# A value scale found ahead of V Wo', keys split in another way, and four idle matmuls, in a fused attention and feed-forward kernel

## The reference, cut to what matters

```python
q = hidden @ Wq.T + bq
scores = einsum('bshd,hmd->bshm', q, memory_keys) / sqrt(128)
probs = softmax(scores)
mem_out = einsum('bshm,hmd->bshd', probs, memory_values)
x = layernorm(x + mem_out @ Wo.T + bo)
...
h = silu(tlin(x, w1)) * tlin(x, w2); h = gelu(tlin(h, h1)); h = gelu(tlin(h, h2))
x = layernorm(x + tlin(h, w3))
```

## Time and the profile before

| | |
|---|---|
| median of 3 runs | 1182.92 us (1181.91 to 1184.15) |
| profiled execution, its own time | 1182.86 us |
| its span in the trace | 1180.9 us |
| mean granted clock of PE | 0.971 |
| busy: PE, DVE, ACT, POOL | 1096.5, 971.5, 901.0, 664.0 us |

### The profile page before, as it was taken

How to read it: one execution, slowest core, us unless ns; L and a number is a source line. 1 busy time by engine, 2 the same in 40 slices (tenths; PEclk the granted TensorE clock), 3 DMA queues, 4 the chain that set the end, 5 groups by cost and what they waited for, 6 DMA issues and landing times. The chain is left out here.

```text
span 1180.9 us, 20085 instructions
## 1 busy us (share of the span) xinstructions
PE 1096.5 (93%) x5312; PEld 758.9 (64%) x5312; DVE 971.5 (82%) x1766; ACT 901.0 (76%) x1582; POOL 664.0 (56%) x614
## 2 busy tenths in 40 slices
PE   7589999999999999999999999643999999999996
PEld 5356666666666666666666666212788888888885
DVE  5868889998999998999899998465678878888875
ACT  5668778887887887887888888613788888888883
POOL 1278787887887887887888787772012112112110
PEclk9889999999999999999999999975999999999998
DMA  5578888888888888888888888812000100101000
GB/s 174 129 167 199 197 190 196 201 196 197 202 196 196 201 197 196 202 196 196 202 196 202 197 198 190 208 65 75 19 28 28 53 27 27 53 27 38 25 10 27
DMA packets 81922, 162.96 MB, mean 138 GB/s; under 512 B 19296, under 2 KB 44768, under 8 KB 81888
## 3 DMA queue, kind: packets, MB, share of 16 engines
q1 hardware_dynamic: 81888, 162.55, 57.9%
HBM read 19.87 MB, written 8.39 MB: 24 GB/s over the span
## 5 line engine op out<-in xcount | busy, mean ns | idle before, releaser
L271 POOL TENSOR_TENSOR pT<-slot_p,pT 128x512 f16<-128x512 f32 x512 | 587.6, 1182 | 139.9 <-ACT pT L310 139.9
L399 DVE TENSOR_SCALAR_CACHE_REDUCE rows<-s_ps 128x1024 f32<-128x1024 f32 x256 | 313.3, 1224 | 76.7 <-PE s_ps L464 62.0
L310 ACT ACTIVATE pT<-slot_p 128x512 f16<-128x512 f32 x512 | 296.9, 616 | 93.4 <-DMA slot_p<-rows 57.3
L363 DVE STREAM_TRANSPOSE rows<-rows 128x1024 f32<-128x1024 f32 x256 | 317.3, 1240 | 2.9 <-ACT rows L301 2.8
L462 PE MATMUL s_ps<-keys,q_buf 128*128 128x512 f32 x512 | 295.6, 577 | 11.6 <-DVE rows L399 6.6
L301 ACT ACTIVATE rows<-rows,bias 128x1024 f32<-128x1024 f32 x256 | 291.6, 1139 | 7.8 <-DVE bias L405 5.6
L489 PE MATMUL o_ps<-pT,v_hi 128*128 128x512 f16 x512 | 201.5, 393 | 34.8 <-POOL pT L271 32.1
L840 PE MATMUL ring<-h_hi,keys 128*128 128x512 f32 x512 | 203.7, 398 | 2.0 <-DVE h_lo L747 1.7
L464 PE MATMUL s_ps<-keys,q_buf 128*128 128x512 f32 x512 | 204.3, 399 | 0.0
L463 PE MATMUL s_ps<-keys,q_buf 128*128 128x512 f32 x512 | 202.8, 396 | 0.0
L841 PE MATMUL ring<-h_lo,keys 128*128 128x512 f32 x512 | 200.5, 392 | 0.0
(11 more groups left out here) (82 smaller groups left out, 1179.7 us busy)
## 6 DMA issues: line engine op xcount, KB each, us to landing
slot_p<-rows SPq DMA_DIRECT2D x1024, 128.0 KB, 2.3
x_in<-in_xT SPq DMA_DIRECT2D x32, 128.0 KB, 2.1
o_scratch<-o_sum SPq DMA_DIRECT2D x32, 128.0 KB, 1.9
o_in<-o_scratch SPq DMA_DIRECT2D x16, 256.0 KB, 2.8
x_in<-in_x SPq DMA_DIRECT2D x16, 256.0 KB, 3.1
out<-y_out SPq DMA_DIRECT2D x16, 256.0 KB, 2.4
slot_p<-in_kT SPq DMA_DIRECT2D x4, 512.0 KB, 6.0
slot_p<-in_vT SPq DMA_DIRECT2D x4, 512.0 KB, 8.4
```

Source lines behind the costliest of these rows:

```text
L271: nc.gpsimd.tensor_tensor(halves(s % RING, 1), slots_first(pp, s), halves(s % RING, 0), ALU.subtract).then_inc(split, 1)
L310: nc.scalar.activation(halves(s % RING, 0), slots_first(pp, s), ACT.Copy).then_inc(highed, 1)
L363: nc.vector.transpose(row_piece(tile, k), row_piece(tile, k)).then_inc(turned, 1)
L399: nc.vector.tensor_scalar(row_piece(tile, k), s_ps[:, j % 2, :], 1.0, None, ALU.mult, ALU.max, accum_out=part_max[:, tile, k:k + 1]).then_ ...
```

## The change

1. **Scale.** The scale is no longer found from v. ACT sums |V| over all slots for each of the 128 input channels while V is loaded (four passes, Abs with an accumulator; what they write goes to pT and isn't read). DVE adds the four. ACT multiplies |Wo'| by these sums per partition, PE multiplies by ones and so adds over the channels, and every partition has for each output column a bound on |V Wo'|. DVE clamps it, keeps the exponent, takes the reciprocal and scales Wo' by it: one power of two for each column instead of one for all. PE transposes the powers, so that column 0 of it is v_unscale per partition.
2. **V.** v comes out of PE scaled. Its eight halves move from steps 8 to 15 of frame 0 to steps 11 to 15 of frame 0 and 0 to 2 of frame 1. ACT copies each twice from PSUM, as 16-bit v_hi and as v_raw; POOL subtracts at once. L334, L337, L386, L417, L258 and L420 to L426 are gone.
3. **Keys.** The first piece is loaded and split in two halves; all low parts are made by DVE: three ahead of its first move, one behind each of the first two. One counting semaphore k_split stands for the four.
4. **PE** does four idle products of wq and x_in into o_ps behind the first query product. The x of pair 1 is loaded after them and behind V in SP's queue.

```diff
+        def value_halves(f, t):
+            step = t - V_STEP + STEPS * f if isinstance(f, int) else -1
+            return (step,) if 0 <= step < HALVES else ()
+        def k_part(t, n):
+            return half_piece(t, n) if n < 2 else piece(t, n - 1)
...
 # SP
+                if is_step(pair, 1):
+                    sp.wait_ge(warmed, 1)
-            for n in range(PIECES):
-                sp.dma_start(piece(k_raw, n), piece(kT, n)).then_inc(k_loaded[n], 16)
+            for n in range(K_PARTS):
+                sp.dma_start(k_part(k_raw, n), k_part(kT, n)).then_inc(k_loaded[n], 16)
             sp.wait_ge(q_projected, 1)
-            load_x(1)
             sp.dma_start(wo[:, :], woT).then_inc(wo_loaded, 16)
             for n in range(PIECES):
                 sp.dma_start(piece(v_in, n), piece(vT, n)).then_inc(v_loaded[n], 16)
+            load_x(1)
...
 # POOL
-            for n in range(1, PIECES, 2):
-                k_low_part(pool, nc.gpsimd, n)
-            nc.gpsimd.memset(v_row_max[:, PIECES:PIECES + 1], V_LEAST).then_inc(v_least_ready, 1)
-            pool.wait_ge(v_row_maxed, PIECES + 1)
-            nc.gpsimd.partition_all_reduce(...)
+            nc.gpsimd.memset(ones[:, :], 1.0).then_inc(ones_ready, 1)
+            pool.wait_ge(ones_ready, 1)
+            nc.gpsimd.affine_select(out=ident[:, :], in_=ones[:, :], ...).then_inc(ident_ready, 1)
             for n in range(HALVES):
                 pool.wait_ge(v_high, n + 1)
-                pool.wait_ge(v_scaled, n + 1)
+                pool.wait_ge(v_copied, n + 1)
...
 # ACT
+            act.wait_ge(wo_loaded, 16)
             for n in range(PIECES):
+                act.wait_ge(v_loaded[n], 16)
+                nc.scalar.activation(pT[:, n, :, :]..., piece(v_in, n), ACT.Abs, accum_out=v_sums[:, n:n + 1]).then_inc(v_summed, 1)
...
-                    if is_step(f, 0) and t >= STEPS - HALVES:
-                        n = t - (STEPS - HALVES)
+                    if is_step(f, 0) and t == 9:
+                        act.wait_ge(v_sum_ready, 1)
+                        nc.scalar.activation(wo_size[:, :], wo[:, :], ACT.Abs, scale=v_sums[:, PIECES:]).then_inc(wo_sized, 1)
+                    for n in value_halves(f, t):
                         act.wait_ge(v_made, n + 1)
+                        nc.scalar.activation(half_piece(v_hi_flat, n), o_ps[:, n % 2, :], ACT.Copy).then_inc(v_high, 1)
                         nc.scalar.activation(half_piece(v_raw, n), o_ps[:, n % 2, :], ACT.Copy).then_inc(v_copied, 1)
-                    if is_step(f, 1) and t >= STEPS - HALVES:
-                        (L334 and L337)
...
 # DVE
-            for n in range(0, PIECES, 2):
-                k_low_part(dve, nc.vector, n)
+            for n in range(3):
+                k_low_part(n)
+            def scale_output_weights():
+                dve.wait_ge(wo_bounded, 1)
+                nc.vector.tensor_scalar(wo_bound[:, :], bound_ps, V_LEAST, None, ALU.max).then_inc(wo_clamped, 1)
+                dve.wait_ge(wo_clamped, 1)
+                nc.vector.tensor_scalar(wo_power..., wo_bound..., EXPONENT, None, ALU.bitwise_and).then_inc(wo_powered, 1)
+                dve.wait_ge(wo_powered, 1)
+                nc.vector.reciprocal(wo_scale[:, :], wo_power[:, :]).then_inc(wo_inverted, 1)
+                dve.wait_ge(wo_inverted, 1)
+                nc.vector.scalar_tensor_tensor(out=wo_scaled[:, :], in0=wo[:, :], scalar=V_TOP, in1=wo_scale[:, :],
+                                               op0=ALU.mult, op1=ALU.mult).then_inc(wo_ready, 1)
...
+                    if is_step(f, 0) and j in (0, 1):
+                        k_low_part(3 + j)
+                    if is_step(f, 0) and j == PIECES - 1:
+                        dve.wait_ge(v_summed, PIECES)
+                        nc.vector.reduce_sum(v_sums[:, PIECES:], v_sums[:, 0:PIECES], AX.X).then_inc(v_sum_ready, 1)
+                    if is_step(f, 0) and j == PIECES:
+                        scale_output_weights()
                     if is_step(f, 1) and j == 0:
+                        dve.wait_ge(power_turned, 1)
+                        nc.vector.tensor_scalar(v_unscale[:, :], turn_ps[:, 0:1], 1.0 / V_TOP, None, ALU.mult).then_inc(unscale_ready, 1)
...
 # PE
+            for n in range(WARMUPS):
+                last = nc.tensor.matmul(o_ps[:, n % 2, 0:2 * P], wq[:, :], x_in[:, :], start=True, stop=True)
+            last.then_inc(warmed, 1)
...
+                        if is_step(f, 0) and tile == 0 and (t == 1 or t % 2 == 0):
+                            pe.wait_ge(k_split, 1 if t == 0 else j + 2)
...
+                    if is_step(f, 0) and t == 9:
+                        pe.wait_ge(ones_ready, 1)
+                        pe.wait_ge(wo_sized, 1)
+                        nc.tensor.matmul(bound_ps, ones[:, :], wo_size[:, :], ...).then_inc(wo_bounded, 1)
+                    for n in value_halves(f, t):
                         if n == 0:
+                            pe.wait_ge(wo_ready, 1)
+                            pe.wait_ge(ident_ready, 1)
+                            nc.tensor.transpose(turn_ps, wo_power[:, :], ident[:, :]).then_inc(power_turned, 1)
                         at_least(pe, v_copied, n - 1)
-                            ... v_in[:, at:at + P], wo[:, :],
+                            ... v_in[:, at:at + P], wo_scaled[:, :],
```

More of the change, by code:

```diff
@@ L44 @@
 PV_LAG = 16
+WARMUPS = 4
 V_TOP = 2.0 ** 14
 V_LEAST = 2.0 ** -100
+V_STEP = 11
+EXPONENT = 0x7F800000
 RING = 8
@@ L51 @@
 CHUNKS = SLOTS // P
+K_PARTS = PIECES + 1
 BT = 512
@@ L109, in attention @@
         table_spare = sb("exp_table_spare", [P, 1], FP32)
-        v_row_max = sb("v_row_max", [P, PIECES + 2], FP32)
-        v_max = sb("v_max", [P, 2], FP32)
-        v_scale = sb("v_scale", [P, 1], FP32)
+        v_sums = sb("v_sums", [P, PIECES + 1], FP32)
+        ones = sb("ones", [P, P], FP32)
+        wo_size = sb("wo_size", [P, P], FP32)
+        wo_bound = sb("wo_bound", [P, P], FP32)
+        wo_power = sb("wo_power", [P, P], FP32)
+        wo_scale = sb("wo_scale", [P, P], FP32)
+        wo_scaled = sb("wo_scaled", [P, P], FP32)
+        ident = sb("ident", [P, P], FP32)
         v_unscale = sb("v_unscale", [P, 1], FP32)
@@ L122, in attention @@
         o_ps = ctx.enter_context(nc.psum_tensor("o_ps", [P, 2, 4 * P], FP32))
-        k_loaded = [sem(f"k_loaded{n}") for n in range(PIECES)]
+        w_ps = ctx.enter_context(nc.psum_tensor("w_ps", [P, 4 * P], FP32))
+        k_loaded = [sem(f"k_loaded{n}") for n in range(K_PARTS)]
         v_loaded = [sem(f"v_loaded{n}") for n in range(PIECES)]
@@ L128, in attention @@
         k_high, v_made, v_high, v_copied, v_split = map(sem, ("k_high", "v_made", "v_high", "v_copied", "v_split"))
-        v_least_ready, v_row_maxed, v_maxed, v_power_ready = map(sem, ("v_least_ready", "v_row_maxed", "v_maxed", "v_power_ready"))
-        v_scale_ready, v_scaled = sem("v_scale_ready"), sem("v_scaled")
-        k_split = [sem(f"k_split{n}") for n in range(PIECES)]
+        ones_ready, ident_ready, v_summed, v_sum_ready, wo_sized = map(
+            sem, ("ones_ready", "ident_ready", "v_summed", "v_sum_ready", "wo_sized"))
+        wo_bounded, wo_clamped, wo_powered, wo_inverted, wo_ready, power_turned, unscale_ready = map(
+            sem, ("wo_bounded", "wo_clamped", "wo_powered", "wo_inverted", "wo_ready", "power_turned", "unscale_ready"))
+        k_split, warmed = sem("k_split"), sem("warmed")
         scored, bias_ready, exped = map(sem, ("scored", "bias_ready", "exped"))
@@ L222, in exchange @@
                         sp.wait_ge(v_split, HALVES)
-                        for n in range(PIECES):
-                            sp.wait_ge(k_split[n], 1)
+                        sp.wait_ge(k_split, K_PARTS)
                     at_least(sp, split, 16 * p - 16)
@@ L292, in _ @@
             q_high_part(0, 0)
+            for n in range(K_PARTS):
+                act.wait_ge(k_loaded[n], 16)
+                nc.scalar.activation(k_part(k_hi, n), k_part(k_raw, n), ACT.Copy).then_inc(k_high, 1)
+            act.wait_ge(wo_loaded, 16)
             for n in range(PIECES):
-                act.wait_ge(k_loaded[n], 16)
-                nc.scalar.activation(piece(k_hi, n), piece(k_raw, n), ACT.Copy).then_inc(k_high, 1)
+                act.wait_ge(v_loaded[n], 16)
+                nc.scalar.activation(pT[:, n, :, :].rearrange("p c n -> p (c n)"), piece(v_in, n), ACT.Abs, accum_out=v_sums[:, n:n + 1]).then_inc(v_summed, 1)
             def exp_piece(p, tile, k):
@@ L476, in frame @@
                             at = n * HALF + c * P
-                            last = nc.tensor.matmul(o_ps[:, n % 2, c * P:(c + 1) * P], v_in[:, at:at + P], wo[:, :],
+                            last = nc.tensor.matmul(o_ps[:, n % 2, c * P:(c + 1) * P], v_in[:, at:at + P], wo_scaled[:, :],
                                                     start=True, stop=True, skip_group_check=True)
```

52 lines of the change are left out of this document (13 added, 39 removed).

## The result

The changed kernel takes 1169.37 us (median of 4 runs, 1167.80 to 1170.08), the kernel before, run beside it, 1182.71 us (4 runs, 1181.91 to 1184.15): a ratio of 0.9881, with a 95% interval of 0.9867 to 0.9895. The profiled execution took 1168.93 us around a span of 1167.1 us. The forecast was 1170.6.

The account below looks back on a forecast made before the run. PE's matmuls bound the loop, so only the start could gain: t=4 of frame 2 from 70.23 to 57.75 us, 12.5 us, less 0.2 for added matmuls and ACT's queue, gives 1170.6 us; range 1167.5 to 1175.5.

Parts of the forecast that it names:

- yardstick: Step t=4 of frame 2, from which PE runs without a hole: forecast to move from 70.23 to 57.75 us.
- gate on V: POOL's pair 0 and SP's pair 1 wait for the last v_lo; first product with V from 63.27 to 52.7 us.
- Keys: Key split at the start, low parts on DVE: fourth move at 17.2 against 17.45 us, worth 0.25 us.
- fourth move: DVE's fourth move of L399 in the first frame, which ends the keys part; forecast at 17.2 us.
- Sums and scale: ACT's Abs passes at Copy's price, reciprocal 0.95 us, three other DVE operations 0.3 each: wo_ready at about 22.85 us.
- V's arrival: V's load at the start: landed soon after 15 us, since only 34 GB/s move from 15 to 20 us.
- Rival (e): Abs passes delay the first exp if V's last piece lands after 17.5 us; 1185.4 us at 32.5; chance 3%.
- Frame 1: Move 1 at 36.3, move 4 at 43.95, first high part at 50.85, first product with V at 52.7 us.
- Rival (a), the clock,: PE enters frame 2's first product at half rate: 1.9 us lost, 1172.5 us, with another spell 1174; chance 25%.
- (b): Scale chain or ACT's queue longer, so V pushes frame 1; 3 us more gives 1173.5 us; chance 14%.
- (c): Abs changes tables or early frames give back: 2.6 us or about as much, 1173.3 us; chance 10%.
- (d): Pair 1's transfers would be late anyway; only frame 1's 1.65 us remain, 1181.2 us; chance 3%.

Follow-up runs that it names:

- scale_only: The change without its key split, idle matmuls and moved load of x, so only the new scale and its V steps; 1171.44 us, ratio 0.9901.
- keys_only: The kernel before with the key halves, all key low parts on DVE, the idle matmuls and the load of x behind V; 1182.80 us, ratio 0.9996.
- held: scale_only with idle matmuls in frame 1 and ahead of the first product with V; 1170.43 us, ratio 0.9887.
- no_idle: The change without the four idle matmuls and SP's wait for them; 1169.81 us, ratio 0.9887.
- inverse: The change with the reciprocal of the powers of two replaced by an integer operation on their bits; 1168.03 us, ratio 0.9863.
- spread: The change with one half of V in every second step instead of in every step; 1167.74 us, ratio 0.9855.
- late16: The change with V's halves in steps 0 to 7 of frame 1 instead of from step 11 of frame 0; 1168.61 us, ratio 0.9870.
- cast_act: The change with the cast of the feed-forward weights at the hand-over made by ACT in three pieces instead of by DVE; 1168.67 us, ratio 0.9873.
- old_keys: The change with four whole key pieces and low parts by DVE and POOL in turn, idle matmuls kept; 1170.81 us, ratio 0.9894.

## Why the prediction was right

**What the yardstick carried.** Of the 13.8 us of span, 12.94 are the shift of t=4, which was forecast at 12.5. That the gain comes from the gate on V is shown by scale_only: the new scale alone takes 11.65 of the 13.3 us, keys_only nothing that can be told.

**Keys.** Forecast: fourth move at 17.2; measured 16.95 us. DVE's queue did take the place of POOL's contention as written; its operations start 1.14 us apart (move 0 at 10.49, move 2 at 15.04), where the sum took their full 1.22 and 1.23. The value of 0.25 us was mis-sized: it was taken against the 17.45 us of one trace, and the old keys part leaves the fourth move to PE's rate, which rises at a different moment in each trace; for the same landings the split is, as estimated above, worth 0.25 (held: 9.67 + 7.60 against 17.52) to 1.1 us. The step that said so, that DVE paces the stretch and PE's rate saves almost nothing, held; its bound, 18.2 us were PE still at half rate in step 6, wasn't put to the test: no_idle had its six scores of steps 0 and 1 at half rate, and the same 7.60 us. PE's scores were on time: the idle matmuls ended at 7.1 us, not at 8.3 (eight recorded rows in 2.95 us, where the sum took 1.02 us for each of the four), and the first key half was there at once, at 6.79.

**Sums and scale.** Abs at the price of Copy: 1.06 us, with no table load around it. By the Trainium skill ("ScalarE: Activation LUTs", Table sets), which has abs in every set, the price was to be nothing; the trace agrees. The reciprocal: 0.95 forecast, 0.95 measured, so 6.2 ns a column holds from 64 to 128. The other three 0.29, 0.23 and 0.29 for 0.3 each. wo_ready at 22.89 for 22.85.

**V's arrival** is the step that came near to failing. The forecast read from a rate of 34 GB/s in 15 to 20 us that V has landed soon after 15 us. ACT's Abs passes start at 13.65, 14.87, 16.15 and 17.44 us, each as its piece lands, so V's last piece is there only at 17.4, and x behind it at 17.7, for which PE waits 0.85 us. Rival (e) had named 17.5 us as the point from which every further microsecond is one of the path. The last Abs ended at 18.50 us and the bias for the first exp was there at 18.55, so V itself was in time by 0.05 us. The moved x was not: the query product waited for it, ACT's query high part (18.49 us) behind that product stands ahead of the first exp, and the exp starts at 18.87, 0.32 us behind the bias. In inverse, where x landed 1 us earlier, it starts at 18.23, 0.03 behind the bias. The gain stood, but the reason given for its safety was wrong: in the kernel before, too, V's last piece is issued at 7.2 us and takes 9.5 to its landing at 16.7, while in 16 to 17 us only 8 GB/s move. The rate of a window doesn't tell when a transfer counts as landed.

**Frame 1.** Move 1 at 36.05 (36.3), move 4 at 43.67 (43.95), first high part at 50.53 (50.85), first product at 52.44 (52.7): each some 0.25 us early. That isn't what the keys part was early: x took that back, and wo_ready and the eighth half of V (34.26 + 1.05 = 35.31 us against 35.3) came as forecast. It is the three scores behind that half, which start at 35.07 us beside it and not at 35.5. That V on PE sets this stretch is shown by spread and late16, that the scale chain does by inverse.

**Rival (a), the clock,** was given 25% and 1.9 us. It is real: 0.9 to 2.5 us in seven of the traces, five of them with the new scale. In the change's own trace it didn't come (4.85 us where the forecast had 5.05), in that of the same start in cast_act it did. So it should have stood not as a rival but as a coin for each run. The forecast's argument that frame 1 is as sparse as before was right, and yet didn't decide it. The kernel before, same window:

```profile
40.00:50.00 10.00, 7.21 (x25) 4.47 (x24) 9.90 (x19) 6.29 (x11) 2.34 (x2) 0.89 0.79 178
```

That is 25 matmuls in 40 to 50 us in both, at a clock that falls towards the end there and stays at 1.00 here.

**(b), (c) and (d)** didn't happen; of (c), a give-back in the early frames, the runs show the reverse: 1.38 us less behind t=4. That stretch varies between 635.8 and 637.0 us in the other kernels, and is 636.28 in keys_only, which keeps the old scale. So it isn't V's, and its cause stays open. With the hand-over's 0.44 less, the feed-forward part's 0.96 more, and 12.94 us at t=4 where the sum counted 12.3, it puts the span 1.5 us under the forecast; the median lies 1.2 under it.

## What to carry to other kernels

Where a scale has to be known before a product is used, a bound from sums of its inputs lets it be applied to the small operand ahead of the product, and every pass over the large result goes; look for the engine whose next stage waits for that pass. Take a moment from which the bound engine never stops as the yardstick, and follow each saving to it: here 12.94 us of the yardstick were 13.3 of the time. Read the landing of the last byte from the instruction that consumes it, not from the rate of a window, and put a load that is moved to the end of a queue on the list of waits. A short stretch whose clock comes out one way in one trace and the other way in the next needs several traces, or a price for both.

## What the runs showed of the hardware

The granted clock of one and the same start came out at 1.00 in one trace and at 0.50 in the next (54 to 56 us, the change and cast_act), which is 4.85 against 6.34 us for four steps. PE had been busy for 6.50 us of 40 to 50 in the first and 6.69 in the second.

A f32 cast of 5632 columns by DVE beside two-input f32 operations of POOL has two outcomes. In the change it takes 3.32 us and the POOL operation beside it 3.99, in inverse it takes 10.41 us and POOL's keep their 1.15 to 1.17. Of the twelve traces that have this cast on DVE, eleven show 3.2 to 4.1 us and one 10.41. In all twelve the cast ends 2.95 us behind the end of a POOL operation: in ten the one that was running when the cast started, in late16 the next, in inverse the last of seven in a row, when POOL's queue had run empty. So 2.95 us are the cast's own time and the rest is a wait, which POOL's operations, one behind the other, can stretch. The Trainium skill ("GPSIMD Engine Reference", Specifications) says that GpSimd shares its SBUF interfaces with DVE's instructions that have two SBUF inputs or run in a mode with two ports; the trace agrees for DVE's two-input operations, since two of POOL's take 3.7 us beside L402 and those beside the one-input reductions 1.15, and for the key low parts too, 1.23 us alone and 2.25 beside POOL's. That the cast runs in such a mode no trace names; by the change's trace a column of it costs 0.52 ns (2.95 us for 5632) and one of the reduction 1.10 (2.82 us for 2560).

The start itself moves between traces: the second whole key piece landed so that its low part began at 8.99 to 9.98 us, and the fourth move at 16.59 to 17.58 with it. When PE's scores go over from one every 0.43 us to one every 0.23 moved too: 12.9 us in held, 13.8 in before and 15.5 in scale_only, whose keys part is the same, and 16.0 in old_keys, which has the idle matmuls ahead of it, each time with PE busy almost without a hole since 9.4 to 9.9 us. And a transfer counts as landed well behind its bytes: V's last piece at 16.7 us in the kernel before, where only 8 GB/s still move in 16 to 17 us. A tenth of a per cent of this kernel is 1.2 us, so differences of parts below that are read from traces with this spread in mind.
